# A four-layer cross-attention kernel on one core: one common order of stages replaced by an order for each engine

## The reference

```python
x = _L0(ctx, x, mask)   # 16 heads; queries from x, keys and values from concat(ctx, x); softmax, out, + x; rmsnorm; gelu MLP 256-1024-256; + x
x = _L1(x, ctx)         # RWKV block: layer norm, token shift mixes, r k v g w, a scan over 64 positions, group norm, gate, Wo; then a channel mix
x = _L2(x, ctx)         # one-head attention of x on ctx, x + alpha * delta
x = _L3(x, ctx, mask)   # 32 query heads on 8 key/value heads; softmax; out + x; layer norm
# the scan of L1, for each of 32 heads with 8 x 8 states:
#   a = k[:, None] * v[None, :];  out = r @ (u * a + s);  s = a + w[:, None] * s
```

## Time and profile before

| what | us |
|---|---|
| median of 3 runs (1621.12 to 1624.65) | 1621.43 |
| span of the profiled execution | 1618.4 |
| PE busy | 1416.4 (88%) |
| PE weight loads busy | 1073.0 (66%) |
| DVE busy | 1076.6 (67%) |
| ACT busy | 622.2 (38%) |
| POOL busy | 626.3 (39%) |

### The profile page before, as it was taken

How to read it: one execution, slowest core, us unless ns; L and a number is a source line. 1 busy time by engine, 2 the same in 40 slices (tenths; PEclk the granted TensorE clock), 3 DMA queues, 4 the chain that set the end, 5 groups by cost and what they waited for, 6 DMA issues and landing times.

```text
span 1618.4 us, 34489 instructions
## 1 busy us (share of the span) xinstructions
PE 1416.4 (88%) x14312; PEld 1073.0 (66%) x14312; DVE 1076.6 (67%) x2073; ACT 622.2 (38%) x1351; POOL 626.3 (39%) x604
## 2 busy tenths in 40 slices
PE   5878999999999999999999999999999999987664
PEld 4656777666777776666777766667777667765443
DVE  2354686866768686776868677686868667774735
ACT  2333444334334443434444443444443343432221
POOL 1061615336261634526162543616153352605210
PEclk9898999999999999999999999999999999997786
DMA  7030313114031312304041221403131130404000
GB/s 288 11 56 14 57 31 46 39 24 71 17 57 31 53 33 33 60 17 63 25 63 31 40 44 23 72 17 57 32 45 40 29 65 17 54 4 57 3 11 7
DMA packets 65787, 70.40 MB, mean 43 GB/s; under 512 B 19808, under 2 KB 54752, under 8 KB 65248
## 3 DMA queue, kind: packets, MB, share of 16 engines
q1 hardware_dynamic: 65632, 68.19, 22.1%
HBM read 30.42 MB, written 4.19 MB: 21 GB/s over the span
## 4 chain that ended last, share of the span: by engine, by line
PE 61%; DVE 15%; ACT 8%; POOL 6%; issue 4%; DMA 4%; SPq 1%; DVEq 0%; POOLq 0%; ACTq 0%
PE pw L411 13%; PE pw L389 12%; PE pw L591 7%; PE pw L597 7%; PE pw L447 4%; PE pw L542 4%; DMA big<-kvrg 4%; PE pw L495 3%; DVE c L1096 3%; PE pw L395 2%; ACT ptA L814 2%; PE pw L400 2%; POOL ab L1039 2%; DVE ab L1250 2%; POOL ab L1003 1%
## 5 line engine op out<-in xcount | busy, mean ns | idle before, releaser
L1250 DVE TENSOR_TENSOR_SCAN ab<-pw,ab 128x256 f32<-128x256 f32 x256 | 160.4, 674 | 107.0 <-ACT ab L924 81.3
L1003 POOL TENSOR_TENSOR ab<-big,kvrg 128x504 f32<-128x504 f32 x128 | 161.5, 1262 | 74.3 <-DMA big<-kvrg 50.9
L1039 POOL TENSOR_TENSOR ab<-ab,kvrg 128x512 f32<-128x512 f32 x128 | 167.7, 1315 | 0.5 <-DVE ab L1250 0.5
L988 POOL TENSOR_TENSOR vtmp_B<-mv_B,eps 128x2 f32<-128x2 f32 x16 | 3.1, 197 | 383.7 <-DVE mv_B L1111 383.7
L1026 POOL TENSOR_TENSOR big<-big,xaB 128x512 f32<-128x512 f32 x80 | 93.3, 1175 | 99.8 <-DVE big L1229 99.8
L389 PE MATMUL pw<-big,wb 128*128 128x256 f32 x512 | 127.8, 393 | 0.2 <-ACT kvrg L897 0.2
L591 PE MATMUL pw<-tA,wb 128*128 128x256 f32 x512 | 125.5, 396 | 2.1 <-DVE tA L1194 2.1
L1229 DVE SCALAR_TENSOR_TENSOR big<-pw,wa,sxB 128x256 f32<-128x256 f32 x160 | 67.0, 478 | 78.1 <-PE pw L495 78.1
L816 ACT ACTIVATE ptC<-pw 128x1024 f32<-128x1024 f32 x64 | 62.1, 1022 | 146.8 <-PE pw L447 146.8
L597 PE MATMUL pw<-wb,ptA 128*128 128x256 f32 x512 | 115.6, 379 | 0.0
L591 PEld LDWEIGHTS pw<-tA,wb 128*128 128x128 f32 x512 | 97.9, 196 | 25.0 <-issue 9.3
(11 more groups left out here) (211 smaller groups left out, 3096.8 us busy)
## 6 DMA issues: line engine op xcount, KB each, us to landing
big<-kvrg SPq DMA_DIRECT2D x256, 128.0 KB, 3.9
hT<-in_h SPq DMA_DIRECT2D x16, 512.0 KB, 4.1
wb<-in_wb SPq DMA_DIRECT2D x1, 5120.0 KB, 21.2
a<-in_x SPq DMA_DIRECT2D x16, 256.0 KB, 2.7
xB<-in_x SPq DMA_DIRECT2D x16, 256.0 KB, 2.7
result<-c SPq DMA_DIRECT2D x16, 256.0 KB, 2.0
m<-in_mask SPq DMA_DIRECT2D x16, 128.0 KB, 2.5
m<-in_amask SPq DMA_DIRECT2D x32, 64.0 KB, 2.3
```

What stands on the lines that cost most here:

```text
L1003: G.tensor_tensor(ab[i % 4][:, :, :, 1:S], vx[i % 3].rearrange("p j (b s) -> p j b s", b=NB)[:, :, :, 0:S - 1], k, ALU.mult).then_inc(kv_p ...
L1039: G.tensor_tensor(ab[i % 4][:, :, :, :], st[i % 2][:, :, :, :], r, ALU.mult).then_inc(pd_ok, 1)
L1250: last = V.tensor_tensor_scan(st[i % 2][:, j, :, :].rearrange("p b s -> p (b s)"), kn(b5)[:, i // 4, :], ab[i % 4][:, j, :, :].rearrange(" ...
```

## The change

`ORDER` and `AHEAD` go. In their place `FLOW` gives each engine three strings of letters: a head of 160 stages (all of A0 to A2, B0, B1, C0), a round of 81 that is taken `STEADY` = 11 times, and a tail of 245 (two tiles of A, three of B, four of C). `sequence(engine)` reads the strings of one engine: each letter takes the next stage of that part, of the tile at which the part then stands. The stages themselves, their instructions, waits and transfers stay as they are, and so do the order within each part and the order of PE's dense stages on ACT and DVE. `numbers()` goes by PE's order, so the turns of banks 6 and 7 and of the attention banks change with it.

```diff
-AHEAD = {"A": 2, "B": 1, "C": 0}
-ORDER = "ABABBABBBABBABBCBABBABBBBBCACBCBBBCCABBCCACBCBBBCAAACBBBBCABCBACAABCAABBCACCCACCC"
+FLOW = {
+    "PE": (
...
+        "ABAABBCBBABBBBBABBBACCCBBABBCBBBBACBACBCACBBCBCAACCBBBBBABBACACAAABBCACACACCBCCBC",
...
+    "DVE": (
...
+        "ABABBBBBBBABBACABABBBBACBCBBBBCACBBCCBABCBCACBACBBAACBCBABBBABCACAACABACABCCCBCCC",
...
+    "ACT": (
...
+        "AABBBBBBABBBBACBABBBBCBBACBCBBABCBACBABBACBCBCAACBCCACBABBCCBABACABBAACCBACBACCCC",
...
+    "POOL": (
...
+        "ABBBBABACBBBABBCCCBABBBBAABBCBCBABBCBCCBBABCACBBAACCBCCBBCCAAABABABAABCBCCACBABCC",
...
+    "SP": (
...
+        "AABBBBCBBBBBBACCBCBABBABABBBBCBABBABBCCACCCBBBBABCABABBCBBCAABCCBCACCAACABCACCCAA",
...
+STEADY = 11
...
-def sequence():
-    out = []
-    for it in range(-AHEAD["A"], TILES):
-        at = {part: iter(STAGES[part]) for part in STAGES}
-        for part in ORDER:
-            name, i = next(at[part])
-            if 0 <= it + AHEAD[part] < TILES:
-                out.append((name, i, it + AHEAD[part]))
+def sequence(engine):
+
+    head, steady, tail = FLOW[engine]
+    at, out = dict.fromkeys(STAGES, 0), []
+    for part in head + steady * STEADY + tail:
+        t, k = divmod(at[part], len(STAGES[part]))
+        at[part] += 1
+        out.append(STAGES[part][k] + (t,))
     return out
...
-    for name, i, t in sequence():
+    for name, i, t in sequence("PE"):
...
-def run(engine, stage):
-    for name, i, t in sequence():
+def run(engine, stage, order):
+    for name, i, t in sequence(order):
         stage(name, i, t)
...
-            run(pe, stage)
+            run(pe, stage, "PE")
```

More of the change, by code:

```diff
@@ L378, in _ @@
             load_context(2)
-            run(sp, stage)
+            run(sp, stage, "SP")
             sp.wait_ge(st_out, 16 * TILES)
@@ L980, in _ @@
             act.wait_ge(set_pool, 2)
-            run(act, stage)
+            run(act, stage, "ACT")
         @block.gpsimd
@@ L1064, in _ @@
             G.memset(power[:, :], -0.5).then_inc(set_pool, 2)
-            run(pool, stage)
+            run(pool, stage, "POOL")
         @block.vector
@@ L1366, in _ @@
             last.then_inc(set_dve, 1)
-            run(dve, stage)
+            run(dve, stage, "DVE")
 def pack(weights, table):
```

31 lines of the change are left out of this document (added).

## The result

The changed kernel takes 1569.8 us in the median, 1621.3 for the kernel before in the same comparison: a ratio of 0.969, 95% interval 0.965 to 0.973.

What follows compares the result with a forecast made beforehand. Rounds were taken as TensorE work with small holes, the ends as bound by chains between engines; head -4, 13 rounds -19.5, tail -7 make -30.5 from the 1618.4 span, 1587.9, plus 3.0 gives 1591 us; range 1558 to 1616.

Steps and rivals of the forecast that it cites:

- rival 1: Deeper overlap: holes of (c), (d), (e), (h) too high; a round gains 4.5 us at most, about 1562; chance 0.13.
- (a): Round's start: v0 between k0 and mix1 covers VectorE's chain, so mix1's hole goes from 0.54 us to 0.
- (b): mix1 and mix20 stay adjacent on TensorE, so the 1.02 us hole ahead of mix20 stays.
- (c): cturn, about 0.5 us, replaces v0 between mix20 and mix22: new hole of 1.3 us ahead of mix22.
- (d): max01 moves behind pk and pw1, its wait 0.2 to 0; turn0 gets a new 0.3 us hole (0 to 0.9).
- (e): Between exp01 and value00, fv gives 1.8 us where ScalarE needs 2.12: new hole of 0.45 us.
- (f): sum1 behind x2turn, GpSimd's products earlier: hole 0.92 us to 0; sum3 behind x3turn: 0.34 to 0.
- (g): l2s with sum1 ahead: 0.79 us to 0.3; l2o stays 0.48; out00 keeps about 0.4; v3 goes to 0.
- (h): x3turn moves ahead of sum2 and sum3 and waits for out0's bank: new hole 0.65 us; zturn 0.47 to 0.4.
- (i): outg moves behind value11: value10 keeps its 1.11 us hole, out11's 0.93 goes to 0.
- 2: Only the ends gain: in the rounds new holes equal the old; head and tail give -4 - 7: 1610 us; chance 0.20.
- 3: Slower: VectorE's serial stretch gnorm1 to mix1 decides once 0.8 us later than listed; at 4 us late 1632; chance 0.10.

Runs made afterwards that it cites:

- outg back: Changed kernel with outg on TensorE, gturn and norm2 on VectorE, norm2 on GpSimd put back or earlier in 11 rounds: 1601.2 us, ratio 0.989.
- new head alone: New order only in the head (A1 with B0, and A2, B1, C0), the common order in rounds and tail: 1607.9 us, ratio 0.993.
- cut tail: Changed kernel, tail cut at tile 15's q0: new order ahead and old behind 1596.0 us, ratio 0.984; the reverse 1572.7, ratio 0.971.
- rounds alone: New order only in the 11 full rounds, the common order in head and tail: 1604.8 us, ratio 0.990.
- the reciprocal: Changed kernel with one more 128x512 reciprocal on VectorE, on an unread buffer, ahead of gnorm1 in 12 rounds: 1592.0 us, ratio 0.986.
- outg and q0 moved: Kernel with l2k moved, plus outg behind exp11 and the next q0 ahead of out11 on TensorE in 11 rounds: 1568.3 us, ratio 0.969.
- l2k moved: Kernel with v0 back, plus l2k of C behind mix1 on TensorE and ScalarE in the same 11 rounds: 1560.1 us, ratio 0.964.
- v0 back: Changed kernel with v0 between mix20 and mix22, cturn behind max00, and ScalarE's k0 behind xturn in 11 rounds: 1561.8 us, ratio 0.966.
- outg late: Kernel with v0 back, plus only outg moved behind exp11 on TensorE, ahead of value10, in the same 11 rounds: 1571.0 us, ratio 0.969.
- GpSimd and the queue on TensorE's order: Changed kernel with GpSimd and the transfer queue taking TensorE's order of the 11 rounds instead of their own: 1572.7 us, ratio 0.970.
- new tail alone: New order only in the tail (A14, A15, B13 to B15, C12 to C15), common order elsewhere: 1593.4 us, ratio 0.985.

## Why the prediction came out as it did

The sign, the place and the range were right: 1569.8 lies in 1558 to 1616, between the forecast and rival 1. But it is nearer to rival 1 (1562) than to the forecast: 21 us below the 1591, and outside the forecast's own 1574 to 1606. The mechanisms named were those of the forecast; head and tail gained more than twice what was put on them. By the steps:

The distance between successive `q0`, which the prediction said would be 91 (it named L838, the line at which ScalarE reads `q0`; TensorE's is L389), is 89.76 undisturbed and 91.4 in the mean of the 11.

**The rounds, -19.5 for 13.** The sum by sites gave 0.9 a round, the walk from start to start 2.3, and 1.5 was taken. Measured at the full clock it is 2.65: the walk was right, and the next `q0`, put at 90.1, comes at 89.76. The sites were sized too high: of 6.4 us of holes forecast 4.9 are there.
- (a) right: mix1 without a wait, at 9.63 for a forecast of 9.2. Most of the difference is k0's wait of 0.31 for VectorE's reading of out1's bank, not foreseen.
- (b), (c) right: 1.01 stays, and the new hole ahead of mix22 is 1.15 for 1.3.
- (d) turn0's hole of 0.3 isn't there. (e) 0.38 for 0.45.
- (f) right: sum1 and sum3 don't wait. The reason given for sum1, GpSimd earlier because the queue is freer, isn't shown by any run; the kernel in which both follow TensorE's new order has no such wait either.
- (g) 0.22 and 0.48 for 0.3 and 0.48; out00's 0.4 isn't there, and the old round's timeline has no wait ahead of out00 either. (h) x3turn's 0.65 isn't there. Not because VectorE is earlier: it reads out0's bank 2.20 us behind out0's start (834.83 against 832.63), 1.99 before. But out0 and v3 keep TensorE busy for 2.9 us, until that read is done.
- (i) right: 1.11 stays and out11's 0.93 goes; the kernel with outg back prices it at 0.94.

The rest of the round's gain is in no hole. TensorE's busy time is 0.8 us less for the same work. A likely reason is that a group with a hole in its midst takes longer by more than the hole: out1 takes 3.06 us in the kernel with outg back (1074.14 to 1077.20), 2.06 without the wait of 1.00, and 1.73 in the changed kernel, where there is none (868.46 to 870.19). By that one case 0.3 us comes with the hole; for the rest of the 0.8 it is not shown.

**The clock.** It was put at "one more or less is a few us" and left out of the sum. It took 11.4 us of the rounds' 29.2. That the 13 rounds came to about the 19.5 of the forecast (17.7 in 11) is therefore two errors against each other: 1.1 a round too little won, 1.0 a round lost to the clock. Here a term was missing, not only its size, and the agreement is luck.

**The head, -4.** Measured -11.1, beyond the bound of -7; the new head alone gave 0.993, the same 11 us. The holes were read rightly: sum0 no longer waits 3.76. In A1 with B0 TensorE's idle time falls from 15.3 to 10.4, near the 4. But its busy time falls too, from 64.19 to 56.85 for 606 and 599 matmuls, at a clock of 0.89 before and 0.95 after. That term was missing. Its size varies: the two other kernels with the old head spend 78.63 and 77.89 us in this stretch, with 16.7 and 17.3 us idle and a clock of 0.91 and 0.93. All with the new head lie between 67.3 and 68.6, with 10.4 idle. So 5 to 7 us of the gain are waits, and the rest, some 3 to 7 us, busy time at a lower clock.

**The tail, -7.** The forecast for the whole stretch from `q0` of tile 14 was -7 and two rounds of -1.5, so -10; measured -24.5, again beyond the bound. From `q0` of tile 15 to mix1 of B15 91.6 us instead of 97.7, with 97 matmuls more done in it: the 4.71 ahead of mix1 is gone, VectorE being in time, as was said. Behind it the forecast counted mainly what stands in B15's way. It let C14 run ahead of B15's scans, but by 5 us at most; how much of C14 B15 can carry was the term put too low: 433 matmuls against 308 lie between mix1 and norm2 of B15, in 0.9 us less time, so norm3 of C14 starts 3.45 us after norm2 instead of 13.02, which is 9.6 of the 24.5. This is read from the traces; the runs with the cut tail show only that the gain comes with the order behind the cut. Idle time of TensorE in the tail fell by 17.0 us (76.8 to 59.7) and busy time by 7.5; B15's stretch has a clock of 0.88 instead of 0.79. C15 alone is unchanged, 74.2 for 74.0, as forecast.

**The rivals.** 1, deeper overlap, said that the holes of (c), (d), (e), (h) were too high; for (d) and (h) it was right, for (c) and (e) it was not, and its 4.5 a round was too much. Nor do its own figures fit together: 2 us left of 7.3 would be 5.3 a round, and 13 x 4.5 = 58 less 4 is 54, which gives 1567 and not 1562. 2 falls, since the rounds alone give 0.990. 4 falls. 3 is sound as a mechanism, with 0.87 us of slack for a forecast 0.8: the reciprocal made each round 2.3 longer. It didn't act, because VectorE comes to xturn 5.3 us after `q0`, exactly as listed. And the contention that the Trainium skill's page "SBUF — State Buffer", section "Who interferes with whom", would make a danger did not grow: VectorE's busy time in a round is 66.34 after and 67.05 before. The price of 0.3 us for each meeting was one row's, though. Beside GpSimd's outer products and products the same instruction took 0.77 to 1.21 us over the 15 tiles before, and 0.89 to 0.93 over the 14 after that meet one. It takes longer the later GpSimd's instruction ends: 0.77 where that ended 0.2 us behind its start (194.26), 1.21 where it ended 0.7 behind (937.90). So the later one waiting for the other's end, as the prediction has it, is borne out.

## What to carry to other kernels

A hole closed in a stretch at a reduced clock can be worth more than its length (here 5 to 7 us less idle time went with 9 to 12 us less in all), and where one engine is nearly full a new hole set beside an old one can cost more than its length: count the clock as a term, from rows at either level. When an order is changed, walk the whole round from start to start instead of adding up holes, and check for each stage moved what it had covered in its old place; outg and l2k only moved a hole. Look for gain at the ends first: the tail, where the last chain came to carry more of the second-last tile, was worth more here than all 11 steady rounds.

## What the hardware showed

TensorE's clock fell in rounds in which it was busy over 94% of the time and no single wait was over 1.2 us; six of the seven disturbed rounds of the changed kernel are such. The seventh, the first of the 11, is the handover from the new head, with a wait of 2.24 us ahead of k0. Slices of a disturbed round of the changed kernel, then the same part of the undisturbed one before it:

```profile
883.00:886.50 3.50, 2.35 (x23) 1.73 (x20) 1.66 (x4) 0.40 (x2) 2.16 (x2) 0.87 0.00 0
886.50:890.00 3.50, 3.50 (x33) 2.66 (x30) 1.88 (x5) 0.00 (x0) 2.45 (x3) 0.50 0.00 0
890.00:893.50 3.50, 3.50 (x12) 2.83 (x11) 3.50 (x6) 0.45 (x1) 3.21 (x4) 0.65 0.00 0
```

```profile
793.20:796.70 3.50, 2.35 (x36) 1.75 (x36) 1.85 (x5) 0.45 (x2) 2.12 (x2) 1.00 0.00 0
```

Both times TensorE has just waited 1.0 us for mix20 and 1.15 for mix22. In the one the granted clock then goes to 0.50, the 1.2 GHz level, for 6.8 us in all (0.9, 3.5 and 2.4 of the three slices) and the round costs 2.8 us more; in the other it stays at 2.4 GHz. The same drop in the kernel before:

```profile
346.00:350.00 4.00, 4.00 (x12) 2.84 (x9) 1.66 (x4) 0.00 (x0) 2.42 (x3) 0.50 0.00 0
```

Where in the round the clock falls is the same each time. Two more rounds, one of the changed kernel (its `q0` at 508.75) and one of the kernel with new rounds alone (789.60), ahead of the fall and in it:

```profile
519.75:523.75 4.00, 1.83 (x16) 1.21 (x14) 1.66 (x4) 2.15 (x9) 0.85 (x1) 1.00 0.00 0
523.85:527.15 3.30, 3.30 (x41) 3.09 (x41) 1.49 (x4) 0.00 (x0) 1.89 (x3) 0.50 0.02 5
```

```profile
800.80:804.80 4.00, 2.02 (x15) 1.42 (x18) 1.66 (x4) 1.95 (x8) 1.06 (x1) 1.00 0.00 0
804.95:815.05 10.10, 10.10 (x58) 7.96 (x53) 6.22 (x12) 0.60 (x1) 6.60 (x6) 0.50 0.01 2
```

Both falls begin 15.0 to 15.3 us behind `q0`, just after mix22's hole. Over the traces of all 14 kernels, the second to the eleventh round show 57 falls. Each begins between 1.1 us before and 1.4 us after the end of a wait of one of two kinds. Either it is the second of two waits close together, with ends 2.0 to 2.9 us apart (1.0 at mix20 and 1.15 at mix22; 0.5 or 1.06 at mix1 and 1.0 at mix20; some 1.0 to 1.3 at sum1 and 0.8 at l2s in the old round), or it is the single wait of 1.92 us ahead of k0 in the kernel with outg and q0 moved. In the kernel with l2k moved, where no such pair stands at the start of the round, these ten rounds show no fall.

Over the kernels, waits of TensorE around the start of a round (from out11 to mix22) and disturbed rounds among the 11:

| kernel | waits, us | disturbed | undisturbed round | 11 rounds |
|---|---|---|---|---|
| l2k between mix1 and mix20 | 1.4 | 1 | 90.4 | 997.3 |
| v0 back | 2.4 | 3 | 89.9 | 998.6 |
| before | 2.5 | 2 | 92.4 | 1023.3 |
| changed | 2.5 | 7 | 89.8 | 1005.6 |
| changed, with the reciprocal | 2.5 | 3 | 92.1 | 1025.8 |
| outg and q0 moved | 3.0 | 6 | 90.8 | 1001.7 |
| outg back | 3.2 | 11 | none | 1035.1 |
| outg late | 3.7 | 5 | 90.4 | 1007.8 |

The kernel with the fewest waits has one disturbed round and a kernel with 3.2 us has all eleven, but the sum of the waits is no rule: three kernels with 2.5 us have 2, 3 and 7, and one with 3.7 has 5. Nor are 2 and 7 the chance of one execution: the four other kernels with the new order in the rounds have 7, 6, 7 and 7 disturbed rounds (new rounds alone, GpSimd and the queue on TensorE's order, the two with the cut tail), the two others with the old order (new head alone, new tail alone) 2 and 2. So the place of a fall is shown, and that their number goes with the kernel and not with the execution; in which of the rounds that all have the pair the clock falls, and why the reciprocal, which adds a wait elsewhere, has fewer falls, stays open.
